# Scores of linear attention: two heads at a time on 32-row quarters of the array, instead of four heads through zero-padded copies of q

## The reference, cut to what matters

```python
def step(S, inp):
    qb, kb, vb = inp
    inter = jnp.einsum('bhcd,bhde->bhce', qb * decay_q[None, :, :, None], S)
    scores = jnp.einsum('bhcd,bhed->bhce', qb, kb) * dmask[None]
    intra = jnp.einsum('bhce,bhed->bhcd', scores, vb)
    S_new = lam_c[None, :, None, None] * S + jnp.einsum('bhcd,bhce->bhde', kb * decay_k[None, :, :, None], vb)
    return (S_new, inter + intra)
```

## Time and profile before

| | |
|---|---|
| median of 3 runs | 2218.04 us (2217.8 to 2221.76) |
| the profiled execution | 2218.5 us |
| its span, first to last instruction | 2216.5 us |
| PE busy | 2000.0 us (90%) |
| DVE busy | 1272.7 us (57%) |
| ACT busy | 962.8 us (43%) |
| mean granted TensorE clock | 0.965 of full speed |
| L940, the copies of Z | 151.1 us of ACT, 512 copies |
| L753, the matmuls of S | 132.5 us of PE in 256 records, two for each float32 matmul |
| L1141, the mask multiplication | 87.4 us of DVE, 128 operations |

### The profile page before, as it was taken

How to read it: one execution, slowest core, us unless ns; L and a number is a source line. 1 busy time by engine, 2 the same in 40 slices (tenths; PEclk the granted TensorE clock), 3 DMA queues, 4 the chain that set the end, 5 groups by cost and what they waited for, 6 DMA issues and landing times.

```text
span 2216.5 us, 28811 instructions
## 1 busy us (share of the span) xinstructions
PE 2000.0 (90%) x10192; PEld 1602.9 (72%) x10192; DVE 1272.7 (57%) x2960; ACT 962.8 (43%) x1946; POOL 266.5 (12%) x310
## 2 busy tenths in 40 slices
PE   6787999999999999999999999999999999996564
PEld 4465677777677776776777677779999999995443
DVE  3545564655555655655755554446666666665676
ACT  4333343433443443443443343346666666662222
POOL 1101001001001001001001002011111111115330
PEclk9898999999999999999999999999999999998787
DMA  7966245454355256254454347357777777757773
GB/s 246 399 218 214 60 146 194 141 169 162 107 171 179 69 182 205 69 186 144 134 190 133 103 137 247 108 194 239 245 247 244 242 243 245 252 186 256 233 261 125
DMA packets 153663, 416.85 MB, mean 188 GB/s; under 512 B 18401, under 2 KB 18545, under 8 KB 146353
## 3 DMA queue, kind: packets, MB, share of 16 engines
q1 hardware_dynamic: 118656, 239.13, 33.7%
q0 software_dynamic: 34432, 175.80, 22.0%
q10 hardware_dynamic: 432, 0.07, 0.0%
HBM read 307.98 MB, written 106.95 MB: 187 GB/s over the span
## 4 chain that ended last, share of the span: by engine, by line
PE 76%; DVE 11%; DMA 6%; issue 3%; ACT 2%; SPq 1%; POOL 0%; DVEq 0%; ACTq 0%
PE banks L690 21%; PE banks L692 20%; PE banks L691 20%; PE banks L753 4%; DMA xT_lo<-xt_scratch 2%; DMA out<-fin_x 2%; PE banks L761 2%; PE banks L765 2%; PE banks L865 2%; DVE fin_shared L1317 1%; PE banks L771 1%; DMA ffn_w_raw<-w_ffn 1%; PE banks L871 1%; PE banks L719 1%; DVE pair_stats L1079 1%
## 5 line engine op out<-in xcount | busy, mean ns | idle before, releaser
L690 PE MATMUL banks<-xT_hi,ffn_gate_up_hi 128*128 128x512 f32 x704 | 307.4, 437 | 73.1 <-DVE hidden_late L1282 40.6
L691 PE MATMUL banks<-xT_lo,ffn_gate_up_hi 128*128 128x512 f32 x704 | 284.8, 404 | 0.0
L692 PE MATMUL banks<-xT_hi,ffn_gate_up_lo 128*128 128x512 f32 x704 | 284.7, 404 | 0.0
L690 PEld LDWEIGHTS banks<-xT_hi,ffn_gate_up_hi 128*128 128x128 f32 x704 | 138.4, 197 | 126.4 <-DVE hidden_late L1282 53.5
L690 PE MATMUL banks<-moe_gu_hi,moe_xT_hi 128*128 128x352 f32 x624 | 215.7, 346 | 3.4 <-DVE moe_xT_lo L1299 3.4
L940 ACT COPY q_one_head<-qT 32x128 f32<-32x128 f32 x512 | 151.1, 295 | 117.8 <-PE banks L753 112.5
L692 PE MATMUL banks<-moe_gu_hi,moe_xT_lo 128*128 128x352 f32 x624 | 201.8, 323 | 0.0
L691 PE MATMUL banks<-moe_gu_lo,moe_xT_hi 128*128 128x352 f32 x624 | 201.3, 323 | 0.0
L1292 DVE TENSOR_TENSOR moe_gu_lo<-moe_gu_raw,moe_gu_hi 128x704 fp32r<-128x704 f32 x156 | 135.1, 886 | 96.7 <-ACT moe_gu_hi L1006 96.7
L691 PEld LDWEIGHTS banks<-xT_lo,ffn_gate_up_hi 128*128 128x128 f32 x704 | 139.1, 198 | 32.4 <-issue 7.4
L692 PEld LDWEIGHTS banks<-xT_hi,ffn_gate_up_lo 128*128 128x128 f32 x704 | 138.0, 196 | 30.9
(11 more groups left out here) (233 smaller groups left out, 4283.1 us busy)
## 6 DMA issues: line engine op xcount, KB each, us to landing
ffn_w_raw<-w_ffn SPq DMA_DIRECT2D x176, 384.0 KB, 3.2
att_w_hi<-att_w_split SPq DMA_DIRECT2D x112, 256.0 KB, 3.7
att_w_lo<-att_w_split SPq DMA_DIRECT2D x112, 256.0 KB, 4.5
x_normed_by_expert<-xT_hi POOLq DMA_DIRECT2D x13, 1536.0 KB, 10.2
moe_x<-x_normed_by_expert SPq DMA_DIRECT2D x78, 256.0 KB, 3.0
expert_out<-moe_y SPq DMA_DIRECT2D x78, 256.0 KB, 2.9
x_in<-x SPq DMA_DIRECT2D x32, 256.0 KB, 4.7
x<-x SPq DMA_DIRECT2D x32, 256.0 KB, 5.3
```

The source lines that it names most:

```text
L690: pe.matmul(out_ap, l_hi, r_hi, start=start, stop=False)
L691: pe.matmul(out_ap, l_hi, r_lo, start=False, stop=False)
L692: return pe.matmul(out_ap, l_lo, r_hi, start=False, stop=stop)
```

## The change

One S piece is now for half of a chunk's heads: `half` takes heads 2·half and 2·half+1 of all four groups. It has 8 float32 matmuls of 32 rows, with 128 weight columns and 128 moving columns, directly from kT and qT, and takes two banks, one for each of the two heads' rows. The matmuls change between the two row quarters. VectorE multiplies the two banks in two operations of 128x512, and the piece counts as done after the second. Z and qz are gone. probsT holds all 16 heads of a chunk in the order head-in-group, group; the mask is ordered accordingly on the host. IP of either half waits for both S pieces. S has two entries in the list of banks. The places are changed, also of pieces that have nothing to do with S.

```diff
 PLACES = {
-    "xin": (-24, -23.77, -23.55, -23.52,),
-    "N1A": (1.77,),
+    "xin": (-21.16, -20.93, -20.71, -20.68,),
+    "N1A": (2.23,),
     "N1B": (3,),
-    "N1": (3.45, 4, 5.45, 6.45,),
-    "T1": (5.2, 6.53, 7.2, 8.2,),
+    "N1": (4.32, 4.49, 5.45, 6.45,),
+    "T1": (5.2, 6.53, 7.2, 9.02,),
...
     "QK": (10, 11, 12, 13.15, 14, 15, 16, 16.71,),
...
-    "Z": (16.22, 18.45, 20.6, 21.3, 25.39, 26.39, 28.54, 28.94, 33.94, 33.63, 36.79, 37.49, 42.17, 43.65, 45.1, 45.87,),
-    "KT": (18, 27.12, 35.35, 42.87,),
-    "S": (19, 20, 22, 23.75, 27.39, 27.94, 30.85, 30.94, 35.49, 36.49, 38.49, 39.49, 43.87, 44.87, 46.87, 47.87,),
+    "KT": (19.42, 27.12, 35.26, 42.87,),
+    "S": (21.42, 23.42, 27.94, 30.85, 36.4, 38.4, 44.89, 46.89,),
     "V": (21.15, 21.85, 23.3, 23.85,),
-    "IP": (21.6, 24.6, 29.39, 31.94, 37.79, 40.49, 46.32, 48.87,),
-    "ST": (25, 32.94, 41.49, 49.87,),
-    "OUT": (28.27, 35.39, 43.94, 50.87,),
-    "LO": (36.6, 51,),
+    "IP": (23.72, 26.02, 31.15, 31.94, 38.7, 40.4, 47.19, 48.89,),
+    "ST": (26.42, 32.94, 41.4, 49.49,),
+    "OUT": (29.69, 35.39, 43.85, 50.89,),
+    "LO": (36.72, 51.02,),
...
-    "xto": (58.7,),
-    "R1": (57.21,),
-    "R2": (58.88,),
+    "xto": (61.71,),
+    "R1": (57.23,),
+    "R2": (59.2,),
...
-    "PG": (66.45,),
+    "PG": (67.7,),
...
 OPENING = {
...
-    "S": (19, 20, 22, 23.75, 27.39, 27.94, 30.85, 30.94, 36.35, 37.35, 39.35, 40.35, 43.87, 44.87, 46.87, 47.87,),
+    "S": (20, 22, 27.94, 30.85, 37.35, 39.35, 44.87, 46.87,),
     "V": (21.15, 21.85, 23.3, 23.85,),
-    "IP": (21.6, 24.6, 29.39, 31.94, 38.65, 41.35, 46.32, 48.87,),
+    "IP": (22.3, 24.6, 31.15, 31.94, 39.65, 41.35, 47.17, 48.87,),
...
-ARGS = {"Z": (NC, G), "S": (NC, G), "IP": (NC, 2)}
+ARGS = {"S": (NC, 2), "IP": (NC, 2)}
...
-BANKED = [p for p in ORDER["P"] if p[0] in
-          ("T1", "QK", "V", "KT", "S", "IP", "ST", "OUT", "T2", "R1", "R2", "RK")]
+BANKED = [(p, i) for p in ORDER["P"] if p[0] in
+          ("T1", "QK", "V", "KT", "S", "IP", "ST", "OUT", "T2", "R1", "R2", "RK") for i in range(1 + (p[0] == "S"))]
...
-        qz = sb("q_one_head", [2, GH, P], scope=phase1)
-        probs = sb("probsT", [2, GH, P], scope=phase1)
+        probs = sb("probsT", [GH, G, P], scope=phase1)
...
             elif kind == "S":
-                c, g = args
-                pe.wait_ge(a_piece, done("A", "Z", a, c, g))
-                mm = pe.matmul(b, kT[:, g, c * P:(c + 1) * P], qz[:, g % 2].rearrange("p h t -> p (h t)"),
-                               start=True, stop=True)
+                c, half = args
+                b2 = pe_bank(pe, piece, 1)
+                if (c, half) == (0, 0):
+                    pe.wait_ge(a_piece, done("A", "QK", a, 7))
+                for g in range(G):
+                    for i in range(2):
+                        r = slice((2 * half + i) * HD, (2 * half + i + 1) * HD)
+                        mm = pe.matmul((b, b2)[i][:, g * P:(g + 1) * P], kT[r, g, c * P:(c + 1) * P],
+                                       qT[r, g, c * P:(c + 1) * P], start=(g == 0), stop=(g == G - 1),
+                                       skip_group_check=True)
             elif kind == "IP":
                 c, half = args
-                pe.wait_ge(v_piece, max(done("V", "S", a, c, 2 * half + 1), done("V", "V", a, c), done("V", "KT", a, c)))
+                pe.wait_ge(v_piece, max(done("V", "S", a, c, 1), done("V", "V", a, c), done("V", "KT", a, c)))
...
-                                       probs[:, g % 2, j, :], start=False, stop=(gl == 1), skip_group_check=True)
+                                       probs[:, j, g, :], start=False, stop=(gl == 1), skip_group_check=True)
...
-            elif kind == "Z":
-                c, g = args
-                if (c, g) == (0, 0):
-                    act.wait_ge(a_piece, done("A", "QK", a, G - 1))
-                if 4 * c + g >= 2:
-                    act.wait_ge(p_piece, done("P", "S", a, *divmod(4 * c + g - 2, G)))
-                for j in range(GH):
-                    r = slice(j * HD, (j + 1) * HD)
-                    op = act.copy(qz[r, g % 2, j, :], qT[r, g, c * P:(c + 1) * P])
...
             elif kind == "S":
-                c, g = args
-                op = ve.tensor_tensor(probs[:, g % 2, :, :], chunked(b), mask[:, GH * g:GH * (g + 1), :], ALU.mult)
+                c, half = args
+                for i in range(2):
+                    j = 2 * half + i
+                    op = ve.tensor_tensor(probs[:, j, :, :], chunked(bank_of(piece, i)), mask[:, j * G:(j + 1) * G, :], ALU.mult)
...
-            ve.memset(qz[:, :, :, :], 0.0).then_inc(const_v, 1)
```

More of the change, by code:

```diff
@@ L68 @@
     "xr": (24, 24.3, 44.45, 44.67,),
-    "Z": (16.22, 18.45, 20.6, 21.3, 25.39, 26.39, 28.54, 28.94, 33.94, 33.63, 36.79, 37.49, 42.17, 43.65, 45.1, 45.87,),
-    "KT": (18, 27.12, 35.35, 42.87,),
-    "S": (19, 20, 22, 23.75, 27.39, 27.94, 30.85, 30.94, 35.49, 36.49, 38.49, 39.49, 43.87, 44.87, 46.87, 47.87,),
+    "KT": (19.42, 27.12, 35.26, 42.87,),
+    "S": (21.42, 23.42, 27.94, 30.85, 36.4, 38.4, 44.89, 46.89,),
     "V": (21.15, 21.85, 23.3, 23.85,),
-    "IP": (21.6, 24.6, 29.39, 31.94, 37.79, 40.49, 46.32, 48.87,),
-    "ST": (25, 32.94, 41.49, 49.87,),
-    "OUT": (28.27, 35.39, 43.94, 50.87,),
-    "LO": (36.6, 51,),
[L77 to L81, removed]
-    "xto": (58.7,),
-    "R1": (57.21,),
-    "R2": (58.88,),
[L85 to L91, removed]
-    "PG": (66.45,),
+    "IP": (23.72, 26.02, 31.15, 31.94, 38.7, 40.4, 47.19, 48.89,),
+    "ST": (26.42, 32.94, 41.4, 49.49,),
+    "OUT": (29.69, 35.39, 43.85, 50.89,),
+    "LO": (36.72, 51.02,),
+    "LN": (38.01, 54,),
+    "L": (38.45, 53.54,),
+    "LX": (39.23, 54.82,),
+    "x1o": (39.67, 41.23, 52.12, 54.32,),
+    "T2": (41.6, 42.6, 56.02, 56.76,),
+    "xto": (61.71,),
+    "R1": (57.23,),
+    "R2": (59.2,),
+    "SM1": (59.44,),
+    "SM2": (60.48,),
+    "SM3": (61.13,),
+    "SM4": (61.64,),
+    "CM": (63.99,),
+    "RK": (64.45,),
+    "sc": (61.87,),
+    "PG": (67.7,),
     "W": (),
@@ L105 @@
     "QK": (10, 11, 12, 13.15, 14, 15, 16, 16.71,),
[1 row of a table removed]
     "KT": (18, 27.12, 36.21, 42.87,),
[1 row of a table removed]
[1 row of a table added]
     "V": (21.15, 21.85, 23.3, 23.85,),
[1 row of a table removed]
[1 row of a table added]
     "ST": (25, 32.94, 42.35, 49.87,),
-    "OUT": (28.27, 35.39, 44.8, 50.87,),
+    "OUT": (28.27, 35.39, 47.1, 50.87,),
 }
-ARGS = {"Z": (NC, G), "S": (NC, G), "IP": (NC, 2)}
+ARGS = {"S": (NC, 2), "IP": (NC, 2)}
 def attention_offsets(a):
@@ L302 @@
 PIECES = schedule()
-PARTS = {"N1A": "V", "N1B": "V", "N1": "A", "W": "AV", "T1": "PAV", "QK": "PA", "V": "PV", "KT": "PV", "Z": "A", "S": "PV",
+PARTS = {"N1A": "V", "N1B": "V", "N1": "A", "W": "AV", "T1": "PAV", "QK": "PA", "V": "PV", "KT": "PV", "S": "PV",
          "IP": "PAV", "ST": "PV", "OUT": "PV", "LO": "V", "LN": "A", "L": "V", "LX": "A", "T2": "PAV", "R1": "PA", "R2": "PV",
@@ L313, with bank_before @@
 PLACE = {e: {p: i + 1 for i, p in enumerate(ORDER[e])} for e in "PAV"}
-BANKED = [p for p in ORDER["P"] if p[0] in
-          ("T1", "QK", "V", "KT", "S", "IP", "ST", "OUT", "T2", "R1", "R2", "RK")]
-ALONE = sum(p in BANKED for p in ORDER["P"][:ORDER["P"].index(("GA", 0))])
+BANKED = [(p, i) for p in ORDER["P"] if p[0] in
+          ("T1", "QK", "V", "KT", "S", "IP", "ST", "OUT", "T2", "R1", "R2", "RK") for i in range(1 + (p[0] == "S"))]
+ALONE = sum(PLACE["P"][p] < PLACE["P"]["GA", 0] for p, _ in BANKED)
 BANK = {p: i % 8 if i < ALONE else 6 + i % 2 for i, p in enumerate(BANKED)}
-def bank_before(piece):
-    i = BANKED.index(piece)
-    return next((p for p in reversed(BANKED[:i]) if BANK[p] == BANK[piece]), None)
+def bank_before(piece, part):
+    i = BANKED.index((piece, part))
+    return next((p[0] for p in reversed(BANKED[:i]) if BANK[p] == BANK[piece, part]), None)
 def last_alone(bank):
-    return next(p for p in reversed(BANKED[:ALONE]) if BANK[p] == bank)
+    return next(p[0] for p in reversed(BANKED[:ALONE]) if BANK[p] == bank)
 def done(engine, *piece):
@@ L533, in pool_piece @@
                 a, i = args
-                pool.wait_ge(p_piece, done("P", "S", a, *divmod(i, G)))
+                pool.wait_ge(p_piece, done("P", "S", a, i // G, i % G // 2))
                 if i == 0:
@@ L692, in three, with bank_of @@
             return pe.matmul(out_ap, l_lo, r_hi, start=False, stop=stop)
-        def bank_of(piece):
-            return ps[:, BANK[piece], :]
+        def bank_of(piece, part=0):
+            return ps[:, BANK[piece, part], :]
         def pe_evicted(pe, old):
@@ L702, in pe_evicted, with pe_bank @@
                 pe.wait_ge(v_piece, done("V", *old))
-        def pe_bank(pe, piece):
-            old = bank_before(piece)
+        def pe_bank(pe, piece, part=0):
+            old = bank_before(piece, part)
             if old:
                 pe_evicted(pe, old)
-            return bank_of(piece)
+            return bank_of(piece, part)
```

(21 more changed lines are left out.)

## The result

The changed kernel is slower: 2321.35 us median of 4 runs (2316.47 to 2321.9) against 2219.9 us (2217.8 to 2223.59), a ratio of 1.045 with a 95% interval of 1.0429 to 1.0472. The forecast was slower, at 2249 us and no more than 2290: the direction held, and of some 101 us it had 31. The profiled execution is 2320.96 us, its span 2318.9 us, and the mean granted clock 0.929 where it was 0.965.

What follows compares the result with a forecast made beforehand. TensorE's streaming and waits were taken to bound the kernel from some 216 to 1280 us. 2218.5 + 34 - 3 = 2249.5, less 0.5 because the profiled execution is over the median, gave 2249 us, range 2199 to 2290.

Steps and rivals of the forecast that it cites:

- What bounds the kernel: From some 216 to 1280 us, time is what TensorE streams plus what it waits; ScalarE is no bound.
- S on TensorE: An S piece costs 1.30 us, eight a block 10.4 instead of 13.8: 3.4 us a block gained, 24 in seven.
- The new waits: TensorE around S in attention: new waits of 12.7 us a block, from two shared banks and the places of pieces.
- kT's waits: TensorE's waits for ScalarE's kT in the interleaved stretch, 5.2 us before, were to go.
- Waits and S together: Per attention block: 12.7 of new waits, less 4.4 of waits gone and 3.4 saved on S: +4.9 us, seven blocks +34.
- the DMA's -3: DMA waits for xT, 11.2 us, stay, but take up some new waits falling just ahead of them: -3 us.
- the products are covered: Rival: feed-forward parts come so that the four first IPs of a block don't wait: 2205 us; chance 0.27.
- The clock: TensorE's clock from 216 to 1280 us stays at 0.98 or above, with nothing for it in the sum.
- a rival of 0.11: Rival: the clock falls in the new waits, one fall a block costing 22 us: 2271 us; chance 0.11.
- The rest: Opening taken as 0, SyncE and GpSimd queues 0, DMA waits for xT -3 us; stages after 1280 us run no S.

Runs made afterwards that it cites:

- the version with parts at all places around S: Changed kernel with one feed-forward part wherever S stands directly behind V, OUT or KT, or V or IP directly behind S: 2226.23 us, ratio 1.0003.
- the exchanged loops: Changed kernel with S's loops over i and g exchanged, so all four groups of one row quarter run before the other's: 2358.8 us, ratio 1.0596.
- full rows: Changed kernel with waits and places kept, every S matmul over all 128 rows instead of 32, scores summed over four heads: 2302.7 us, ratio 1.0347.
- two row halves: Changed kernel with waits and places kept, each S matmul on 64 rows instead of 32, two side by side: 2294.96 us, ratio 1.0319.

## Why the prediction was wrong

- **What bounds the kernel**: held. TensorE's stream and waits in the interleaved stretch hold 97 of 102 us; ScalarE's 147 us less of busy time are worth nothing.
- **S on TensorE, 1.30 us a piece**: held. Where a feed-forward part surrounds it (the version with parts at all places around S) S starts 0.32 us behind the last matmul's start instead of 0.23, the next starts 1.09 later, and the one after that 0.34 behind it instead of 0.23: 0.09 + 1.09 + 0.11 = 1.29. That is the median of 52 pieces at full clock. Side by side is shown by the row of 1.16 us against the 1.68 of the exchanged loops; in the piece at 651.41 the 16 matmul records start in pairs 6 to 7 ns apart, from the second pair on one every 0.11 us. The Trainium skill's rule ("TensorE: Matmul & The Clock Gate", Part 3), that a load overlaps only with matmuls of another row group, would have given 1.76 us, as the prediction worked out; the trace disagrees with it here, with 1.09 us side by side and 1.60 one quarter after the other. The same part also has a load pulled ahead when it goes to a background weight buffer; what was measured fits that.
- **The new waits**: held nearly to the number. S to IP 28 times, 46.5 us; V to S 14 times, 17.0; S to V 7 times, 9.7; OUT to S 19 times where 15 were counted, 17.9. Together 13.0 us a block; 12.7 had been worked out with the ends of records in it, 11.2 without. kT's waits fell from 5.2 to 1.7 us.
- **Waits and S together**: the terms gave +34 and, with the DMA's -3, +31. Measured in the stage, with the estimate for the clock taken off: 97.3 - 68.7 = +28.6. The coverage that the rival "the products are covered" needed did not exist in this order. Forced, it brings the kernel back to the time before (ratio 1.0003) and not to the 2205 of that rival, as the waits move.
- **The clock: the step that failed.** The forecast said "The clock in 216 to 1280 us stays at 0.98 or above", kept it out of its sum, and gave it to a rival of 0.11 at one fall a block, 22 us. What the runs showed in its place: the clock fell 35 times in the stage, where it had fallen 5 times before the change, and over 180 to 1330 us it was 0.93 for 0.99. By the estimate above that cost 68.7 us in the stage, the greater part of what the forecast lacked. The reasoning had been that "waits of 0.9 to 1.4 us left records at full speed behind them". That was true of a kernel in which full-row work stood around each wait. It was carried over to one in which a piece on two row quarters stands next to the wait. The change made both, and the runs show that either alone costs little: 18 us more at half clock than before from the waits with full rows, 23 from the quarters with parts between, and 144 from both. In the kernel before, the shortest wait with a fall at it was 1.9 us; in this one most of those of 1.5 us behind S had one.
- **The rest**: 5 us. The opening ends at 179 us, before at 180. What comes behind the stage is 5.1 us longer; in its first 680 us, 18.0 us of busy time are at half clock where it was 6.1. Why was not looked into.

What stays open is how much of the difference between two row halves (99 us at half clock) and full, undivided pieces (48 us) is length and how much division. The kernel before with nothing but longer waits of IP wasn't tried. In the kernels with 64 or 128 rows the scores are other numbers too; whether the numbers themselves bear on the clock wasn't tried either.

## What to carry to other kernels

Where TensorE is the bound, a saving that puts its pieces back to back with their own consumers must be counted with the clock: waits beside a half-empty array cost as much again here by the clock as by their own length, some 69 us each. Look at what the array does beside a wait, and not at the wait alone, before carrying over from one kernel to another that waits of a certain size leave the clock alone. And a part pushed into one gap is taken from another: of 91 us of waits removed by order, idle time fell by 45.

## What was not expected of the hardware

The number of array rows that a float32 matmul uses changes how long TensorE runs at half clock, in the same order of work: 174 us with two matmuls of 32 rows side by side, and 99 with two of 64, in pieces of the same length. With 32 rows one at a time, in pieces 0.5 us longer, it is 221. A wait of 1.5 us behind such a piece had a fall of the clock 26 times of 31 with 32 rows, and 3 times of 31 with 128. Its speed otherwise doesn't depend on whether 32 or 64 rows are used: a piece of eight takes 1.16 us in both divided forms. Two matmuls on different row quarters, writing all partitions of two banks, run side by side, also in float32: eight in 1.09 us, against 1.78 us for eight of 128 rows.
